# Products that write nothing needed, put around the round-end products of a five-round scan

## What is computed

```python
def step(state, bc):
    b_t, c_t = bc
    s = state @ A_bar + b_t
    s = _layernorm(s, ln_st_g, ln_st_b)
    return (s, c_t * s)
...
moe_out = jnp.einsum('ebsd,bse->bsd', eo, w_dense)
for i in range(NROT):
    moe_out = moe_out @ expm(gens[i])
...
g = _silu(_L0_ffn_ref(xn, ...))
x = x + s * g
```

## Time and profile before

| | |
|---|---|
| timed executions | 391.05, 392.11, 394.93 us (median 392.11) |
| profiled execution, its own time | 391.37 us |
| its span in the profile | 389.5 us |
| TensorE busy (products) | 323.7 us, 83% |
| VectorE busy | 285.1 us, 73% |
| ScalarE busy | 190.8 us, 49% |
| GpSimd busy | 162.1 us, 42% |
| mean granted clock of TensorE | 0.907 of 2.4 GHz |

### The profile page before, as it was taken

How to read it: one execution, slowest core, us unless ns; L and a number is a source line. 1 busy time by engine, 2 the same in 40 slices (tenths; PEclk the granted TensorE clock), 3 DMA queues, 4 the chain that set the end, 5 groups by cost and what they waited for, 6 DMA issues and landing times.

```text
span 389.5 us, 11592 instructions
## 1 busy us (share of the span) xinstructions
PE 323.7 (83%) x4002; PEld 250.0 (64%) x4014; DVE 285.1 (73%) x1320; ACT 190.8 (49%) x563; POOL 162.1 (42%) x225
## 2 busy tenths in 40 slices
PE   1886988967988869999989999889999988878770
PEld 0676975667555547887777887667767746656450
DVE  2787546999388776888857665669899755788972
ACT  1142982500033325666637668458776628565310
POOL 8051000016777777777776554335554500000000
PEclk9998995865599988999989999889999988999996
DMA  8449990001511314767757667946665224000102
GB/s 276 96 138 199 171 143 0 2 3 34 200 56 57 112 56 162 248 228 248 240 179 234 229 223 241 329 141 210 226 204 211 70 68 164 29 29 29 40 18 87
DMA packets 44158, 54.80 MB, mean 141 GB/s; under 512 B 6841, under 2 KB 28768, under 8 KB 44096
## 3 DMA queue, kind: packets, MB, share of 16 engines
q1 hardware_dynamic: 38975, 42.52, 37.7%
q0 software_dynamic: 4544, 9.39, 7.5%
q10 hardware_dynamic: 576, 2.10, 1.5%
HBM read 14.15 MB, written 16.63 MB: 79 GB/s over the span
## 4 chain that ended last, share of the span: by engine, by line
PE 59%; DVE 24%; issue 5%; ACT 5%; DMA 3%; SPq 2%; DVEq 0%; ACTq 0%
PE bank L1086 11%; PE bank L1527 11%; PE bank L1537 8%; PE bank L1557 2%; PE bank L1490 2%; DVE wT L987 2%; PE bank L1520 2%; PE bank L1505 2%; PE bank L1497 2%; DMA record<-experts 2%; PE bank L459 2%; PE bank L419 2%; PE bank L1426 2%; PE bank L1512 2%; PE bank L445 1%
## 5 line engine op out<-in xcount | busy, mean ns | idle before, releaser
L1748 POOL DMA_INDIRECT token_rows<-rows_out,token_rows_i x78 | 75.7, 971 | 64.2 <-ACT rows_out L1659 27.4
L1086 PE MATMUL bank<-Mrep,wT 32*32 32x64 f32 x2368 | 65.4, 225 | 17.9 <-DVE wT L987 17.6
L1086 PEld LDWEIGHTS bank<-Mrep,wT 32*32 32x32 f32 x2368 | 41.7, 107 | 55.5 <-issue 53.3
L1734 POOL DMA_INDIRECT sorted_rows<-late,slots x64 | 62.7, 980 | 28.4 <-issue 14.5
L1652 ACT ACTIVATE desk<-bank,record 128x128 f32<-128x128 f32 x156 | 48.8, 364 | 44.5 <-PE bank L1527 44.1
L1527 PE MATMUL bank<-desk,record 128*128 128x128 f32 x312 | 58.6, 313 | 0.1
L999 DVE SCALAR_TENSOR_TENSOR ring<-bank,Rho,Dv 128x64 f32<-128x64 f32 x112 | 31.8, 284 | 26.8 <-PE bank L1086 24.4
L1537 PE MATMUL bank<-record,desk 128*128 128x129 f32 x312 | 50.3, 285 | 0.0
L1527 PEld LDWEIGHTS bank<-desk,record 128*128 128x128 f32 x312 | 43.1, 200 | 7.9 <-issue 1.2
L1537 PEld LDWEIGHTS bank<-record,desk 128*128 128x128 f32 x312 | 43.4, 201 | 0.2
L1644 ACT ACTIVATE desk<-bank,cols 128x128 f32<-128x128 f32 x78 | 35.9, 460 | 3.0 <-PE bank L1520 3.0
(11 more groups left out here) (333 smaller groups left out, 635.9 us busy)
## 6 DMA issues: line engine op xcount, KB each, us to landing
record<-experts SPq DMA_DIRECT2D x78, 290.5 KB
sorted_rows<-zero_rows SPq DMA_DIRECT2D x2, 2515.5 KB, 28.3
desk<-sorted_rows SPq DMA_DIRECT2D x26, 193.5 KB
pulls<-token_rows SPq DMA_DIRECT2D x8, 516.0 KB, 5.4
X<-in_L_attn_x ACTq DMA_DIRECT2D x4, 512.0 KB, 6.2
out<-xT SPq DMA_DIRECT2D x8, 256.0 KB, 2.0
token_rows<-rows_out,token_rows_i POOLq DMA_INDIRECT x78
experts<-in_L_ffn_ew SPq DMA_DIRECT2D x1, 1024.0 KB, 6.4
```

What stands on the lines that cost most here:

```text
L1086: t = pe.matmul(psY[q], wT[q, 32 * c:32 * c + 32], Mrep[q, c, :], start=(c == 0), stop=(c == 1))
L1734: pool.indirect_dma_start(sorted_rows[h], bass.IndirectOffsetOnAxis(ap=slots[:, j, q:q + 1], axis=0), sort_rows[:, q, :], None)\
L1748: pool.indirect_dma_start(token_rows[h], bass.IndirectOffsetOnAxis(ap=token_rows_i[:, g:g + 1], axis=0), rows_out[:, g % OUT_PLACES, :], N ...
```

## The change

At the end of each of the first four rounds three such products are put ahead of the two shift products and five behind. In the first round they write bank 2, in the others bank 6, whose earlier contents must have been read by then; hence the added waits on `abel` and `abel_rows`. The end of the fifth round is as it was.

```diff
                     if k == L - 1:
+                        if 0 < r < ROUNDS - 1:
+                            pe.wait_ge(sem("abel_rows"), sum(at <= t for at in ROWS_AT))
+                            if r < 3:
+                                pe.wait_ge(sem("abel"), sum(at <= t for at in ABEL_AT))
+                        if r < ROUNDS - 1:
+                            keep_warm(3, 6 if r else 2)
                         tensor_boundary(pe, turn + 1)
+                        if r < ROUNDS - 1:
+                            keep_warm(5, 6 if r else 2)
```

## The result

| | before | changed |
|---|---|---|
| executions | 22 | 22 |
| median | 394.83 us | 390.07 us |
| lowest to highest | 388.82 to 396.94 us | 386.76 to 392.05 us |
| mean of all, worked out from them | 393.89 us | 390.07 us |
| profiled execution, its own time | 391.37 us | 389.72 us |

The ratio of the changed kernel to the one before is 0.9944, with a 95% interval from 0.9917 to 0.9971: 0.56% faster. This comparison leaves out executions more than 1.5% above the fastest of the same kernel, which is 12 of the 22 of before (those over 394.65) and none of the changed kernel's; over all executions the means stand at 390.07 / 393.89 = 0.990. The forecast was 388.0 us.

A forecast was written before the change was run, and what follows sets the result against it. TensorE, holding 59% of the chain that ended last, was taken as the bound, slowed by low clock behind round ends. 391.37 us - 3.72 (falls avoided) + 0.35 (added products) = 388.0 us, range 385.6 to 391.8.

The forecast's parts named there:

- What the pauses do: At the round ends TensorE idles and the clock falls behind; products that write nothing needed count as activity.
- The cost of the eight products: At the first four round ends: 0.15 us late at the first, about 0.2 at the third; sum 0.35 us.
- The price of a fall: Steps behind the four round ends: low clock costs 1.80, 1.64, 1.22 and 1.28 us, together 5.94 us.
- The page's shorter way: At the round ends: throttled time times one minus the clock's ratio, 17.0 x 0.5 = 8.5 us.
- How often the ends fall: Falls counted at 80% for the first round end, 55% for the three others, giving a gain of 3.72 us.
- What comes next where a stall goes: Second round's GpSimd queue: round can come forward some 1.3 us before `rows_copied` waits; first end's 1.44 us nearly whole.
- the sign that the prediction named for this: Second round: if L1659 begins to wait for the DMA, the prediction is wrong; no size given.
- rival B: Second round: gain reappears as `rows_copied` waiting, or the clock falls a few steps later; 390.1 us, chance 0.25.
- The starting point: Whole kernel: the sum starts from the profiled execution's 391.37 us, 0.7 us under the median of the runs shown, 392.11.

The follow-up runs named there:

- fill_mix: Changed kernel plus five more products behind the first summed rows at t = 127 and t = 132 in the last round; ratio to before 0.9877, median 387.60 us.
- doubled: Changed kernel with six products ahead and ten behind instead of three and five; ratio to before 1.0079, median 396.04 us.
- before_again: The kernel before, unchanged, run against itself with a second trace; ratio 1.0012.
- few_columns: Changed kernel with the same eight products and waits, but 8 columns each instead of 512; ratio to before 1.0022.
- first_only: Changed kernel with the eight products only at the end of the first round; ratio to before 0.9942.
- ahead_only: Changed kernel with only the three products ahead of the shift products, none behind; ratio to before 0.9978.
- behind_only: Changed kernel with only the five products behind the shift products, none ahead; ratio to before 0.9956.
- more_both: Changed kernel plus six products behind t = 79's C projection and three ahead of the state transposes of t = 122, 126, ... 146; ratio to before 0.9903.

## Why the forecast was wrong, point by point

**What the pauses do: right.** The clock falls behind a round's end for want of columns, products that write nothing needed hold it, and 8 columns instead of 512 undo the effect. At ends with all eight products the clock fell in 1 of 21 (fill_mix, first end) and in 1 of 4 of doubled; at ends without a filler of 512 columns in 13 of 15, counted below.

**The cost of the eight products: right.** Forecast 0.15 us at the first end and 0.2 at the third; measured 0.19 and 0.17, and nothing at the others. The price per product held in the doubled version too.

**The price of a fall: right.** The prices from the steps were 1.80, 1.64, 1.22 and 1.28 us, 5.59 in all after the cost. The pair of traces gives 1.74, 1.46, 1.38 and 1.37 with the cost in it, 5.95. The page's shorter way, 8.5 us for TensorE: Matmul & The Clock Gate (Terms) of the Trainium skill, was too much; of the 17.0 us of low clock about 6 came back, since VectorE's share of a step isn't slower at the low clock (L999 takes 0.28 us at either level).

**How often the ends fall: wrong.** I counted the first end at 80% and the others at 55%, because the fifth end had passed a similar pause. That passing was one outcome of two: in 7 of the 12 traces the clock fell within 4.1 us of the last L999 behind the same pause, the changed kernel's first trace among them (at 375.5 us). At the ends that had no filler of 512 columns (in before, before_again, few_columns, and the last three ends of first_only), the first fell 3 times of 3, the second 4 of 4, the third 2 of 4, the fourth 4 of 4: 13 of 15. The 3.72 us were too small a gain at the ends: with the traces of these unfilled ends averaged (13.11, 10.35, 10.28 and 9.10 us) the changed kernel's two traces are 5.5 us shorter over the four ends, costs included, where the sum had 3.72 - 0.35 = 3.4.

**What comes next where a stall goes: wrong place. This is the step of the sum that failed.** I looked for the loss in the second round's GpSimd queue. There ScalarE waited 0.5 us in one trace and 2.2 in the other, none of it seen in the steps; the sign that the prediction named for this (L1659 begins to wait) came, and cost nothing. The loss came in the last round, which the sum put at nothing: a fall at t = 132 or 133, in all six traces that kept the clock at the second, third and fourth ends and had no filler at t = 132 (changed twice, ahead_only, behind_only, more_both, doubled), 6.8 us long in five of them and 3.4 in doubled. It is in none of the four others without a filler there (before, before_again, few_columns, first_only); two of these four fell at t = 140 instead. In the first pair of traces it is worth 2.9 us; against the mean of the four, 31.52 us from t = 131 to 147, the changed kernel's two traces lose 2.2. So by the traces about 5.5 - 2.2 = 3.3 us are left of the change. I did have the clock falling later (rival B), but behind the first end, and only 5.95 - 2.88 - 0.49 - 0.56 = 2.0 us are left of the first pair, of which 1.7 shows in the spans; the rest lies in small shifts between.

**The starting point: wrong as well, and at the level of the time it is the larger error.** The sum went out from one execution of 391.37 us and left open how it stands to the others, with three timed runs to go by. The 22 executions of before have the mean 393.89: not the 0.7 us to the median of three were left out, but 2.5 us. What made that execution quick can be read off. Every execution has its mean granted clock, and as there are two levels its low time is 2 x (1 - clock) x span: 72.6 us for the profiled one. In the 87 executions of before that ran beside the experiments it lies between 65 and 98 us, 81.1 in the mean, and the span is longer by 0.29 us for each us of it (correlation 0.89). By this slope the 8.5 us less are worth about 2.5 us, an estimate.

**How the errors add up.** By the means of all executions the change gave 3.8 us where the sum had 3.4: too little at the ends and nothing for the last round nearly cancel, by luck, and the starting point makes 388.0 out of what was 390.07. By the comparison's 0.56% it gave 2.2 us; then the gain itself fell 1.2 us short of the forecast. By either, the fall in the last round is missing from the sum. That 390.07 lies inside the stated range, and next to rival B's 390.1, is luck: B's mechanism cost nothing in the steps.

**What stays open.** Why the fall of t = 132 comes so regularly with the later round ends in order; six traces show that it goes along, none what it depends on. And what decides how long the clock is low in a given execution: executions of before lie up to 8 us apart, the changed kernel's 5 us. Low time goes with most of this in before (correlation 0.89) and with less of it in the changed kernel (0.61 over its 22 executions).

## What to carry to other kernels

- A short pause of TensorE costs a second time when the clock falls behind it. Price the fall by the steps behind it, at either level, and not by the length of the low stretch; then see whether products without use fit into the pause itself: inside it they cost nothing here (at the second end the first product started 0.39 us after its transpose with and without them), outside they cost 0.22 us each.
- When a fall is taken away, look for the next thin stretch down the program. The first fill gave 5.9 us at its places and kept 1.7 in its trace; the fill at the next thin place may give another half per cent, which isn't shown.
- Where executions scatter by 2% and a profile is one of them, ask for the spread before the sum is anchored on that one, compare its mean granted clock with that of the others, and give the forecast as a difference.

## What was not expected of the hardware

- The same pauses at times brought the clock down and at times not (the third end, unfilled, in 2 of 4 traces; t = 79 in one of the two traces of before), and a low stretch was 3.4, 6.8 or 10.2 us long, with TensorE busy for 87% (5.93 of 6.80, 8.83 of 10.20 us) to all of it (3.40 of 3.40).
- The clock could fall behind the first round's end with all the products in place, in 2 of 7 traces (fill_mix at 145.4 us, doubled at 145.9), so a filler in the pause isn't always enough there.
- Neither three products nor five held the first end, either held the three later ones in its trace.
- A us of low clock cost 0.29 us of span over 87 executions of before, and 5.95 of 17.0 us (0.35) at the four ends.
